# Attention, the sum over the pieces of V in four column groups, and the place at which the maxima are split

## The chip, the cores and the metric

The kernel runs on one core of a Trainium2 chip. Five engines work side by side: TensorE multiplies matrices (PE in the rows; PEld is its weight load), VectorE (DVE), ScalarE (ACT) and GpSimd (POOL) work element by element, and SyncE (SP) issues DMAs. They meet only at semaphores. The metric is the time of one execution on the device in microseconds; several runs give a median.

## What is computed

A layer of linear attention with a normalisation, then a transformer block with softmax attention and a mixture of experts. The change lies in the softmax attention, over 4096 tokens, 16 heads of 16 columns:

```python
scores = jnp.einsum('bqhd,bkhd->bhqk', q, k) / jnp.sqrt(jnp.float32(Dh))
attn = jax.nn.softmax(scores, axis=-1)
ctx = jnp.einsum('bhqk,bkhd->bqhd', attn, v).reshape(Bb, Ss, Dd)
```

(The reference states it for its own batch shape; here it is one sequence of 4096.) The query and key projections are scaled up, so the softmax needs its maxima subtracted, and all of it is done in pieces whose sum is precise.

## The kernel before

`softmax_attention` works through a ring of 128 chunks: 16 heads by 8 chunks of 512 queries. A chunk has 16 slots, one for each unit t; a unit is 128 keys of either half of the keys (k = 0 and 1). Each engine has its own hand-written order, and everything that follows is set by these orders and the semaphores between them.

**TensorE**, in slot t of chunk c: `scores` (L701) makes the scores of unit t, keys by queries, in s_ps (two buffers); `max_pair` (L693) makes scores of chunk c + 2 (LEAD = 2), queries by keys, in two banks of m_ps, only for their maxima; `values` (L720, L726) adds the products of the exponentials with V in o_ps. The visits of `values` lag behind: VISITS and SLOTS say that units 0 and 1 are added in slot 10, unit 3 in slot 12, and so on to unit 15 in slot 24, which is slot 8 of the next chunk. Slots 9 and 11 have no visit. A unit is added either from float32 exponentials (units 3, 6, 9, 12, 15, L720, each matmul in two passes) or from a bfloat16 high part and a float16 low part (L726). The two halves k go to two column groups of 64 in o_ps; each group holds three pieces of V of 16 rows and a row of sums. In slot 11 comes `turn_o` (L735), "the turn" in this text: one float32 matmul, 128 by 128 weights (o_here is the moving data of 512 columns, `gather` the weights), which adds the pieces and both halves up. Its 17 useful rows (16 of the context, one of sums) go to partitions 0 to 16 of m_ps.

**m_ps** has three banks, used in turn: block b, counted over a chunk, uses bank b % 3. The maxima of unit t are blocks 2t and 2t + 1 for t up to 11, the turn is block 24 (TURN_BLOCK), later units come one further. TensorE may write block b when VectorE has read block b - 3.

**VectorE** reads each block of maxima with a reduction (L824); for the units in RELU_PAIRS (2, 5, 8, 12, 15) ScalarE first takes one of the two through a ReLU (L777) and VectorE does the rest in one instruction (L818). Behind slot 11 it copies the turn's result to ctx_stage (L832). In slot 0 it finishes the maxima of the chunk before (tile_max, L839), in slot 6 (FINISH_SLOTS) it transposes their split parts (L842), from which SP fills rows of q_stage.

**ScalarE** takes the exponential of each unit (L790), the ReLUs, and behind slot 8 (COPY_SLOT) copies o_ps to o_here (L781).

**GpSimd** makes the low part of each unit that isn't in FULL_UNITS (L640): 0, 1, 2, 4, 5, 7, 8, 10, 11, 13, 14. MAX_PLACE says ahead of which of them it splits the maxima of the next chunk (L628, L629, L631; `split_max`, which first waits for tile_max): with 2 that is ahead of unit 2. Ahead of the low parts of a head's second chunk it splits V of a later head (`split_v`, L609 to L620); this happens at 14 heads (the first two are done ahead of the ring).

**SP** issues per chunk six loads of queries (L535), 16 row DMAs (L545) once VectorE has transposed, then the two stores of the chunk before (L549, L551), and once per head nine loads of keys.

Of the kernel before, what the change touches and what calls it, by code (L numbers as in the profile page):

```python
# [13 lines left out]
ds = bass.ds  # L14

P = 128
# [3 lines left out]
CHUNK = 512  # L20
CHUNKS = TOKENS // CHUNK
TPC = CHUNK // P
PROJ = 64
HEADS, DH = 16, 16
# [19 lines left out]
O_COLS = DH + 1  # L44
# [6 lines left out]
RING = HEADS * CHUNKS  # L51
Q_BUFS = 4
LEAD = 2
SQ = 32
# [12 lines left out]
COPY_SLOT, TURN_SLOT = 8, 11  # L67
RELU_PAIRS = (2, 5, 8, 12, 15)
FINISH_SLOTS = (0, 6)
MAX_PLACE = 2  # L70
RING_BLOCKS = 2 * UNITS + 1
TURN_BLOCK = 2 * TURN_SLOT + 2
SPLIT_OPS = 5 + len(FULL_UNITS)
# [392 lines left out]
def softmax_attention(nc, dram, keep):  # L466

    with ExitStack() as ctx:
        def sb(name, shape, dt=F32):
            return ctx.enter_context(nc.sbuf_tensor(name, shape, dt))  # L470

        def ps(name, shape, dt=F32):
            return ctx.enter_context(nc.psum_tensor(name, shape, dt))

        def sem(name):
            return ctx.enter_context(nc.semaphore(name))
# [10 lines left out]
        gather = sb("gather", [P, P])  # L487
# [7 lines left out]
        max_parts = sb("max_parts", [P, MROWS, SQ], F32R)  # L495
        max_turned = sb("max_turned", [P, MROWS, SQ])
        o_here = sb("o_here", [P, CHUNK])
        ctx_stage = sb("ctx_stage", [O_COLS, 2, CHUNK])

        s_ps = ps("s_ps", [P, 2, 2, CHUNK])  # L500
        m_ps = ps("m_ps", [P, 3, CHUNK])
# [12 lines left out]
        o_copied, o_turned = sem("o_copied"), sem("o_turned")  # L514
        dve_passed, pool_passed = sem("dve_passed"), sem("pool_passed")
        ctx_out = [sem("ctx_out0"), sem("ctx_out1")]
# [4 lines left out]
        @block.sync  # L521
        def _(sp):
            def load_head(h, par):
                for side, at in ((0, 0), (1, TOP_ROW)):
                    for n, part in enumerate(K_PARTS):
                        sp.dma_start(k_ring[at + DH * n:at + DH * n + DH, ds(par, 1), :].bitcast(F32).rearrange("r a k -> r (a k)"),
                                     dram["ks"][part, ds(h * DH, DH), side, :]).then_inc(head_in, 16)
                for n, part in enumerate(K_PARTS):
                    sp.dma_start(kd_ring[DH * n:DH * n + DH, ds(par, 1), :].bitcast(F32).rearrange("r a k -> r (a k)"),
                                 dram["kd"][part, ds(h * DH, DH), :]).then_inc(head_in, 16)  # L530

            def load_q(h, qc, buf):
                for at in (0, TOP_ROW):
                    for n, part in enumerate(Q_PARTS):
                        sp.dma_start(q_stage[at + DH * n:at + DH * n + DH, ds(buf * CHUNK, CHUNK)].bitcast(F32),  # L535
                                     dram["qs"][part, ds(h * DH, DH), ds(qc * CHUNK, CHUNK)]).then_inc(q_in, 16)

            def rows(n, buf):
                sp.wait_ge(max_ready, n + 1)
                for at in (0, TOP_ROW):  # L540
                    for r in range(MROWS):
                        row = q_stage[at + SROWS + r:at + SROWS + r + 1, ds(buf * CHUNK, CHUNK)].bitcast(F32)
                        row = row.rearrange("a (t b n) -> a t b n", t=TPC, b=P // SQ)
                        for b in range(P // SQ):
                            sp.dma_start(row[:, :, b, :], max_turned[SQ * b:SQ * b + TPC, r, :]).then_inc(rows_in, 16)  # L545

            def store(n, b, h, qc):
                sp.wait_ge(m_read, n * RING_BLOCKS + ((LEAD + 1) * RING_BLOCKS + TURN_BLOCK + 1))
                sp.dma_start(dram["ctx"][ds(qc, 1), ds(h, 1), :, :].rearrange("a b c x -> (a b c) x"),  # L549
                             ctx_stage[0:DH, b, :]).then_inc(ctx_out[b], 16)  # L550
                sp.dma_start(dram["z"][ds(h * CHUNKS + qc, 1), :], ctx_stage[DH:O_COLS, b, :]).then_inc(ctx_out[b], 16)  # L551

            sp.wait_ge(ones_set, 1)
            load_head(sp.snap(0), sp.snap(0))
            for i in range(LEAD + 1):
                load_q(sp.snap(0), i, i)
            rows(0, 0)

            def chunk(h, qc, loads=True, more=True, ahead=True, before=True):

                i = sp.snap(h * CHUNKS + qc)
                if loads:
                    sp.wait_ge(s_done, i * UNITS + 1)
                    n = qc + LEAD + 1
                    load_q(sp.snap(h + n // CHUNKS), n % CHUNKS, n % Q_BUFS)
                    if more and qc == 0:
                        load_head(sp.snap(h + 1), sp.snap((h + 1) & 1))
                if ahead:
                    rows(i + 1, (qc + 1) % Q_BUFS)
                if before:  # L570
                    store(i - 1, 1 - qc % 2, sp.snap(h - 1) if qc == 0 else h, (qc - 1) % CHUNKS)

            for qc in range(CHUNKS):
                chunk(sp.snap(0), qc, before=qc > 0)
            with sp.Fori(1, HEADS - 1) as h:
                for qc in range(CHUNKS):
                    chunk(h, qc)
            for qc in range(CHUNKS):
                chunk(sp.snap(HEADS - 1), qc, loads=qc + LEAD + 1 < CHUNKS, more=False, ahead=qc + 1 < CHUNKS)
            store(RING - 1, 1, sp.snap(HEADS - 1), CHUNKS - 1)  # L580
            for b in range(2):
                sp.wait_ge(ctx_out[b], 32 * (RING // 2))

        @block.gpsimd
        def _(pool):
# [38 lines left out]
            def split_max(n):  # L624

                pool.wait_ge(max_ready, n)
                pool.wait_ge(tile_max_done, n + 1)
                nc.gpsimd.tensor_tensor(neg_max[:, :], no_max[:, :], tile_max[:, :], ALU.subtract).then_inc(max_split, 1)  # L628
                nc.gpsimd.tensor_tensor(max_parts[:, 0, 0:TPC], no_max[:, :], tile_max[:, :], ALU.subtract).then_inc(max_split, 1)  # L629
                pool.wait_ge(max_split, n * 3 + 2)  # L630
                nc.gpsimd.tensor_tensor(max_parts[:, 1, 0:TPC], neg_max[:, :], max_parts[:, 0, 0:TPC].bitcast(F32), ALU.subtract  # L631
                                        ).then_inc(max_split, 1)

            def split_probs(i, more=True):

                for t in POOL_UNITS:
                    if more and t == POOL_UNITS[MAX_PLACE]:
                        split_max(i + 1)
# [32 lines left out]
        def _(pe):  # L671
# [59 lines left out]
            def turn_o(it, c):  # L731

                pe.wait_ge(o_copied, it * PAIR + c)
                pe.wait_ge(m_read, it * (PAIR * RING_BLOCKS) + ((c + LEAD) * RING_BLOCKS + TURN_BLOCK - 2))
                nc.tensor.matmul(m_ps[:, TURN_BLOCK % 3, :], gather[:, :], o_here[:, :], start=True, stop=True  # L735
                                 ).then_inc(o_turned, 1)

            def chunk(it, c, ahead):
                if ahead:
# [25 lines left out]
            for visit, slot in enumerate(SLOTS):  # L765
                if slot >= UNITS:
                    values(HEADS // 2 - 1, PAIR - 1, visit)
            turn_o(HEADS // 2 - 1, PAIR)

        @block.scalar  # L770
# [34 lines left out]
        def _(dve):  # L805
# [21 lines left out]
            def copy_ctx(i, b, stores):  # L827

                dve.wait_ge(o_turned, i)
                if stores is not None:  # L830
                    dve.wait_ge(ctx_out[b], stores * 32)
                nc.vector.tensor_scalar(ctx_stage[:, b, :], m_ps[0:O_COLS, TURN_BLOCK % 3, :], 1.0, None, ALU.mult  # L832
                                        ).then_inc(m_read, 1)

            def finish_max(n, b, step):
# [832 lines left out]
def program(nc, dram):  # L1668
# [6 lines left out]
    with ExitStack() as whole:  # L1675
# [11 lines left out]
        with ExitStack() as through_routing:  # L1687
            keep["v_all"] = right(through_routing, "v_all", [P, TILES, D])
            with ExitStack() as first:
                keep["x_all"] = left(first, "x_all", [P, TILES, D])  # L1690
                linear_attention(nc, dram, keep)
            softmax_attention(nc, dram, keep)
            keep["x_all"] = left(whole, "x1_back", [P, TILES, D])
            output_projection(nc, dram, keep)
            routing(nc, dram, keep)


            keep["w1_in"] = left(whole, "w1_in", [P, HALVES, FF])
            keep["w2_in"] = left(whole, "w2_in", [P, FT, D])
            for name in ("w1_high", "w1_low"):  # L1700
                keep[name] = left(whole, name, [P, 2, HALVES, FT, P], F32R)
            for name in ("w2_high", "w2_low"):
                keep[name] = left(whole, name, [P, 2, FT, D], F32R)
            dispatch(nc, dram, keep)
# [31 lines left out]
```

## Time and profile before

| | |
|---|---|
| runs | 4357.15 us, median of 3 (4355.73 to 4363.25) |
| the profiled execution | 4349.05 us, of which the span is 4347.1 |
| PE busy | 3934.0 us (90%) |
| POOL busy | 3413.5 us (79%) |
| ACT busy | 2829.4 us (65%) |
| DVE busy | 2750.1 us (63%) |
| L735, the turn | 256 passes, mean 686 ns |
| the attention stage | from about 380 to 3472 us of the span |

The span is the time from the first to the last instruction of the profiled execution; what is left of its 4349.05 us lies around it. Times in the rows are microseconds from the start of the span. A row of the order of time gives start, length, engine, line, operation, output and inputs, shapes, the count of merged instructions, and in brackets the idle time ahead of it on its engine with what ended it. Matmuls overlap, so the step from one start to the next is what a matmul costs, and not its own length.

### The profile page before, as it was taken

The page shows a single profiled execution, that of the slowest core. Times are in us where ns is not written, and L with a number is a line of the kernel's source. Part 1 is how long each engine was busy: PE and PEld are TensorE (multiplying, and loading weights), DVE is VectorE, ACT ScalarE, POOL GpSimd, SP SyncE. Part 2 cuts the span into 40 slices and gives each one's busy share as a digit, 9 for nine tenths or more (in the row PEclk, how much of TensorE's full clock was granted, in tenths as well). Part 3 has the DMA queues.
Part 4 walks back from the last instruction along what each step waited for, and adds up shares of the span by engine and source line. Part 5 has one row for each costly group of instructions (what it writes and reads, how often), then busy time and mean ns, then how long its engine had stood idle before and what let it go on. Part 6 is the DMA issues. An engine that isn't in the chain of part 4 may idle for free. (4 is left out here: it accounts for less than half of the span.)

```text
span 4347.1 us, 74722 instructions
## 1 busy us (share of the span) xinstructions
PE 3934.0 (90%) x21172; PEld 1901.6 (44%) x21172; DVE 2750.1 (63%) x5522; ACT 2829.4 (65%) x3421; POOL 3413.5 (79%) x2261
## 2 busy tenths in 40 slices
PE   7469999999999999999999999999999970999990
PEld 4234333333333333333333333333333360899990
DVE  2537777777777777777777777777777451333335
ACT  2125878777787878777787878777788710555550
POOL 0015898989888898988888898988988826888865
PEclk8677999999999999999999999999999975999995
DMA  2241011010101011010101011010100053443434
GB/s 86 111 137 19 11 21 22 10 22 10 22 10 22 10 22 21 11 21 10 22 10 22 10 22 21 11 21 12 20 11 10 17 186 109 140 144 132 147 101 121
DMA packets 145717, 205.12 MB, mean 47 GB/s; under 512 B 43536, under 2 KB 108432, under 8 KB 140176
## 3 DMA queue, kind: packets, MB, share of 16 engines
q1 hardware_dynamic: 127072, 173.76, 14.9%
q0 software_dynamic: 6336, 16.79, 1.2%
q10 hardware_dynamic: 12144, 12.06, 0.8%
q8 instruction: 141, 2.31, 0.2%
q14 instruction: 24, 0.20, 0.0%
HBM read 134.59 MB, written 66.85 MB: 46 GB/s over the span
## 5 line engine op out<-in xcount | busy, mean ns | idle before, releaser
L640 POOL TENSOR_TENSOR probs_low<-probs 128x1024 f16<-128x1024 f32 x1408 | 2632.3, 1894 | 331.0 <-ACT probs L790 324.6
L790 ACT ACTIVATE probs<-s_ps 128x1024 f32<-128x1024 f32 x2048 | 2081.7, 1026 | 240.3 <-PE s_ps L701 190.5
L824 DVE TENSOR_REDUCE unit_max<-m_ps 128x1 f32<-128x512 f32 x2816 | 1779.0, 683 | 222.4 <-PE m_ps L693 181.7
L701 PE MATMUL s_ps<-q_stage,k_ring 50*128 50x512 f32 x4096 | 1043.0, 504 | 1.2 <-DMA q_stage<-max_turned 0.9
L693 PE MATMUL m_ps<-k_ring,q_stage 48*128 48x512 f32 x3456 | 959.5, 424 | 64.3 <-DMA q_stage<-qs_dram 25.4
L701 PEld LDWEIGHTS s_ps<-q_stage,k_ring 50*128 50x128 f32 x4096 | 388.5, 186 | 1160.0 <-issue 907.8
L818 DVE CUSTOM_DVE_ANT_0 excess<-m_ps,excess 128x512 f32<-128x512 f32 x640 | 442.8, 692 | 550.5 <-ACT excess L777 543.9
L720 PE MATMUL o_ps<-probs,v_full 128*64 128x512 f32 x2560 | 698.0, 624 | 0.0
L777 ACT ACTIVATE excess<-m_ps 128x512 f32<-128x512 f32 x640 | 382.1, 597 | 449.8 <-PE m_ps L693 449.8
L726 PE MATMUL o_ps<-probs,v_parts 128*64 128x512 bf16 x2816 | 586.3, 413 | 0.9 <-POOL probs_low L640 0.7
L693 PEld LDWEIGHTS m_ps<-k_ring,q_stage 48*128 48x128 f32 x3456 | 514.8, 192 | 160.5 <-DVE unit_max L824 113.8
L726 PE MATMUL o_ps<-probs_low,v_parts 128*64 128x512 f16 x2816 | 543.2, 383 | 0.0
L1565 DVE TENSOR_TENSOR hidden_low<-h_ps,hidden_high 128x512 fp32r<-128x512 f32 x184 | 127.3, 692 | 365.7 <-ACT hidden_high L1529 365.7
L726 PEld LDWEIGHTS o_ps<-probs,v_parts 128*64 128x64 bf16 x2816 | 156.1, 108 | 379.0 <-issue 304.2
L1525 ACT ACTIVATE h_ps<-h_ps,b_here 128x512 f32<-128x512 f32 x184 | 121.3, 659 | 255.1 <-PE h_ps L1462 255.0
L693 PE MATMUL m_ps<-kd_ring,q_stage 48*128 48x512 f32 x640 | 258.3, 404 | 1.2 <-DVE unit_max L824 1.2
L587 POOL MEMSET k_ring<- 114x4096 f32 x1 | 3.5, 3516 | 293.0 <-POOLq L114 293.0
L1474 PE MATMUL y_ps<-w_low,hidden_high 128*128 128x256 f32 x736 | 209.0, 284 | 0.0
L1474 PE MATMUL y_ps<-w_high,hidden_high 128*128 128x256 f32 x736 | 207.4, 282 | 0.0
L1474 PE MATMUL y_ps<-w_high,hidden_low 128*128 128x256 f32 x736 | 206.6, 281 | 0.0
L720 PEld LDWEIGHTS o_ps<-probs,v_full 128*64 128x64 f32 x2560 | 127.6, 135 | 174.2 <-issue 173.6
L1421 POOL TENSOR_TENSOR w_high<-w_in,zero 128x1024 fp32r<-128x1024 f32 x44 | 130.5, 2983 | 68.3 <-PEq L1493 60.8
(198 smaller groups left out, 3586.6 us busy)
## 6 DMA issues: line engine op xcount, KB each, us to landing
w_in<-in_W SPq DMA_DIRECT2D x46, 1024.0 KB, 4.9
q_stage<-max_turned SPq DMA_DIRECT2D x2048, 0.5 KB
q_stage<-qs_dram SPq DMA_DIRECT2D x768, 32.0 KB, 1.8
k_ring<-ks_dram SPq DMA_DIRECT2D x96, 128.0 KB, 4.2
slots_dram<-zero_rows SPq DMA_DIRECT2D x24, 512.0 KB, 6.3
rows_e<-slots_dram SPq DMA_DIRECT2D x24, 512.0 KB, 3.9
y_slots_dram<-y_out ACTq DMA_DIRECT2D x23, 512.0 KB, 4.3
qs_dram<-parts SPq DMA_DIRECT2D x16, 512.0 KB, 2.8
```

The lines of the kernel that those rows point to most:

```text
L640: nc.gpsimd.tensor_tensor(probs_low[:, LOW_UNITS.index(t), :, :], probs[:, t, :, :], high_view[:, t, :, :, 1], ALU.subtract).then_inc(pool ...
L693: nc.tensor.matmul(m_ps[:, b % 3, :], q_stage[at:at + SROWS, col:col + P], ring[at:at + SROWS, par, key:key + CHUNK], start=True, stop=Tru ...
L701: last = nc.tensor.matmul(s_ps[:, t % 2, k, :], k_ring[at:at + AROWS, par, P * t:P * t + P], q_stage[at:at + AROWS, buf * CHUNK:buf * CHUN ...
L720: last = nc.tensor.matmul(o_ps[V_COLS * k:V_COLS * k + V_COLS, :], v_full[:, par, FULL_UNITS.index(t), k, :], probs[:, t, k, :], start=Fal ...
L726: last = nc.tensor.matmul(o_ps[V_COLS * k:V_COLS * k + V_COLS, :], v_parts[:, par, first_tile(t) + 2 * k, :], part[:, k, :], start=(first ...
L777: nc.scalar.activation(excess[:, :], m_ps[:, block_of(t, 0) % 3, :], ACT.Relu).then_inc(excess_ready, 1)
L790: nc.scalar.activation(probs[:, t, :, :], s_ps[:, t % 2, :, :], ACT.Exp).then_inc(exp_done, 1)
L818: nc.vector.tensor_tensor_reduce(excess[:, :], m_ps[:, block_of(t, 1) % 3, :], excess[:, :], 1.0, LEAST, ALU.add, ALU.max, unit_max[:, b, ...
L824: nc.vector.tensor_reduce(unit_max[:, b, qt, 2 * j + k:2 * j + k + 1], m_ps[:, block_of(t, k) % 3, :], AX.X, ALU.max).then_inc(m_read, 1 + ...
L1421: nc.gpsimd.tensor_tensor(w1_high[:, b, half, :, :], w1[:, half, :, :], zero[:, :].unsqueeze(2).to_broadcast([P, FT, P]), ALU.add).then_in ...
L1474: last = nc.tensor.matmul(y_ps[:, b, t // 2, D * (t % 2):D * (t % 2) + D], h[:, f % 4, cols], w[:, b, f, :], start=(f == 0 and n == 0 and ...
L1565: nc.vector.tensor_tensor(hidden_low[:, f % 4, :], h_ps[:, f % 2, :], hidden_high[:, f % 4, :].bitcast(F32), ALU.subtract).then_inc(low_do ...
```

## The change

MAX_PLACE goes from 2 to 0: GpSimd splits the maxima ahead of the low part of unit 0. The turn becomes four matmuls, each with the first 32 columns of `gather` as weights and a quarter (128 columns) of o_here as data; quarter t goes to the 32 partitions from 32t on. VectorE copies all 128 partitions by 128 columns, and SP stores four pieces of the context and one of the sums (five DMAs in place of two).

```diff
--- before.py
+++ after.py
@@ -67,7 +67,7 @@
 COPY_SLOT, TURN_SLOT = 8, 11
 RELU_PAIRS = (2, 5, 8, 12, 15)
 FINISH_SLOTS = (0, 6)
-MAX_PLACE = 2
+MAX_PLACE = 0
 RING_BLOCKS = 2 * UNITS + 1
 TURN_BLOCK = 2 * TURN_SLOT + 2
 SPLIT_OPS = 5 + len(FULL_UNITS)
@@ -495,7 +495,7 @@
         max_parts = sb("max_parts", [P, MROWS, SQ], F32R)
         max_turned = sb("max_turned", [P, MROWS, SQ])
         o_here = sb("o_here", [P, CHUNK])
-        ctx_stage = sb("ctx_stage", [O_COLS, 2, CHUNK])
+        ctx_stage = sb("ctx_stage", [P, 2, P])
 
         s_ps = ps("s_ps", [P, 2, 2, CHUNK])
         m_ps = ps("m_ps", [P, 3, CHUNK])
@@ -546,9 +546,11 @@
 
             def store(n, b, h, qc):
                 sp.wait_ge(m_read, n * RING_BLOCKS + ((LEAD + 1) * RING_BLOCKS + TURN_BLOCK + 1))
-                sp.dma_start(dram["ctx"][ds(qc, 1), ds(h, 1), :, :].rearrange("a b c x -> (a b c) x"),
-                             ctx_stage[0:DH, b, :]).then_inc(ctx_out[b], 16)
-                sp.dma_start(dram["z"][ds(h * CHUNKS + qc, 1), :], ctx_stage[DH:O_COLS, b, :]).then_inc(ctx_out[b], 16)
+                for t in range(TPC):
+                    sp.dma_start(dram["ctx"][ds(qc, 1), ds(h, 1), :, P * t:P * t + P].rearrange("a b c x -> (a b c) x"),
+                                 ctx_stage[SQ * t:SQ * t + DH, b, :]).then_inc(ctx_out[b], 16)
+                sp.dma_start(dram["z"][ds(h * CHUNKS + qc, 1), :].rearrange("a (t x) -> (a t) x", t=TPC),
+                             ctx_stage[DH:P:SQ, b, :]).then_inc(ctx_out[b], 16)
 
             sp.wait_ge(ones_set, 1)
             load_head(sp.snap(0), sp.snap(0))
@@ -579,7 +581,7 @@
                 chunk(sp.snap(HEADS - 1), qc, loads=qc + LEAD + 1 < CHUNKS, more=False, ahead=qc + 1 < CHUNKS)
             store(RING - 1, 1, sp.snap(HEADS - 1), CHUNKS - 1)
             for b in range(2):
-                sp.wait_ge(ctx_out[b], 32 * (RING // 2))
+                sp.wait_ge(ctx_out[b], 16 * (TPC + 1) * (RING // 2))
 
         @block.gpsimd
         def _(pool):
@@ -732,8 +734,10 @@
 
                 pe.wait_ge(o_copied, it * PAIR + c)
                 pe.wait_ge(m_read, it * (PAIR * RING_BLOCKS) + ((c + LEAD) * RING_BLOCKS + TURN_BLOCK - 2))
-                nc.tensor.matmul(m_ps[:, TURN_BLOCK % 3, :], gather[:, :], o_here[:, :], start=True, stop=True
-                                 ).then_inc(o_turned, 1)
+                for t in range(TPC):
+                    last = nc.tensor.matmul(m_ps[SQ * t:SQ * t + SQ, TURN_BLOCK % 3, 0:P], gather[:, 0:SQ],
+                                            o_here[:, P * t:P * t + P], start=True, stop=True)
+                last.then_inc(o_turned, 1)
 
             def chunk(it, c, ahead):
                 if ahead:
@@ -828,8 +832,8 @@
 
                 dve.wait_ge(o_turned, i)
                 if stores is not None:
-                    dve.wait_ge(ctx_out[b], stores * 32)
-                nc.vector.tensor_scalar(ctx_stage[:, b, :], m_ps[0:O_COLS, TURN_BLOCK % 3, :], 1.0, None, ALU.mult
+                    dve.wait_ge(ctx_out[b], stores * (16 * (TPC + 1)))
+                nc.vector.tensor_scalar(ctx_stage[:, b, :], m_ps[:, TURN_BLOCK % 3, 0:P], 1.0, None, ALU.mult
                                         ).then_inc(m_read, 1)
 
             def finish_max(n, b, step):
```

## Rows read from the trace of the kernel before

**Rows 1.** The page: granted TensorE clock in 40 slices of the span, in tenths.
```profile
PEclk8677999999999999999999999999999975999995
```

**Rows 2.** Order of time, the turns of three chunks.
```profile
401.24 1.12 PE L735 MATMUL m_ps<-o_here,gather 128*128 128x512 f32 x2
...
567.17 1.12 PE L735 MATMUL m_ps<-o_here,gather 128*128 128x512 f32 x2
...
3297.20 1.13 PE L735 MATMUL m_ps<-o_here,gather 128*128 128x512 f32 x2
```

**Rows 3.** Windows: stretch, length, busy PE, PEld, DVE, ACT, POOL (instructions), clock, DMA share, GB/s.
```profile
1519.57:1543.31 23.74, 23.60 (x132) 9.26 (x131) 18.08 (x35) 19.10 (x23) 21.04 (x15) 1.00 0.41 61
1543.31:1571.27 27.96, 26.34 (x132) 10.48 (x131) 18.17 (x35) 19.51 (x23) 25.70 (x24) 0.90 0.04 9
...
1565.40:1572.30 6.90, 6.90 (x24) 2.99 (x22) 3.50 (x8) 3.56 (x4) 6.90 (x4) 0.51 0.01 1
...
2716.70:2742.50 25.80, 23.87 (x132) 9.47 (x130) 18.15 (x35) 19.18 (x23) 23.54 (x23) 1.00 0.04 10
```

**Rows 4.** Order of time, a head's second chunk, POOL, then DVE, then PE.
```profile
1558.86 3.74 POOL L640 TENSOR_TENSOR probs_low<-probs 128x1024 f16<-128x1024 f32 x2 [0.40 <-POOL v_parts L620]
...
1562.57 0.20 POOL L628 TENSOR_TENSOR neg_max<-no_max,tile_max 128x4 f32<-128x4 f32 x1
...
1559.58 1.29 DVE L824 TENSOR_REDUCE unit_max<-m_ps 128x1 f32<-128x512 f32 x2
...
1563.23 0.24 DVE L842 STREAM_TRANSPOSE max_turned<-max_parts 128x64 f32<-128x64 f32 x1 [2.36 <-POOL max_parts L631]
...
1564.11 0.49 PE L693 MATMUL m_ps<-k_ring,q_stage 48*128 48x512 f32 x1 [1.62 <-DVE unit_max L824]
```

**Rows 5.** Line L842, 540 to 3330 us: idle before it (us, times).
```profile
  POOL max_parts L631: 33.2, 14
```

**Rows 6.** Order of time on PE, slots 8 to 12 of an ordinary chunk.
```profile
1538.69 1.08 PE L720 MATMUL o_ps<-probs,v_full 128*64 128x512 f32 x4
...
1541.65 0.41 PE L726 MATMUL o_ps<-probs,v_parts 128*64 128x512 bf16 x2
...
1542.99 0.39 PE L693 MATMUL m_ps<-k_ring,q_stage 48*128 48x512 f32 x2
1543.31 1.13 PE L735 MATMUL m_ps<-o_here,gather 128*128 128x512 f32 x2
1544.37 0.51 PE L701 MATMUL s_ps<-q_stage,k_ring 50*128 50x512 f32 x2
1544.70 0.39 PE L693 MATMUL m_ps<-kd_ring,q_stage 48*128 48x512 f32 x1
```

**Rows 7.** Order of time, slot 0 of the same chunk, POOL, then DVE.
```profile
1528.38 3.75 POOL L640 TENSOR_TENSOR probs_low<-probs 128x1024 f16<-128x1024 f32 x2 [0.44 <-ACT probs L790]
...
1528.62 0.17 DVE L839 TENSOR_REDUCE tile_max<-unit_max 128x4 f32<-128x32 f32 x1
```

**Rows 8.** Order of time on PE, eight transposes in the stage of the experts.
```profile
3736.63 1.04 PE L1454 MATMUL tr_ps<-ident,rows_e 128*128 128x128 f32 x8
```

**Rows 9.** Order of time, slots 10 to 12, DVE, then PEld.
```profile
1543.41 1.29 DVE L824 TENSOR_REDUCE unit_max<-m_ps 128x1 f32<-128x512 f32 x2 [0.45 <-PE m_ps L693]
1544.62 0.67 DVE L832 TENSOR_SCALAR ctx_stage<-m_ps 17x512 f32<-17x512 f32 x1
...
1541.22 0.18 PEld L693 LDWEIGHTS m_ps<-k_ring,q_stage 48*128 48x128 f32 x1 [0.57 <-DVE unit_max L824]
...
1544.76 0.18 PEld L693 LDWEIGHTS m_ps<-k_ring,q_stage 48*128 48x128 f32 x1
```

**Rows 10.** Order of time on SP's queue, end of a chunk's issues.
```profile
1547.51 0.34 SPq L549 DMA_DIRECT2D ctx_dram<-ctx_stage  x1
1548.06 0.24 SPq L551 DMA_DIRECT2D z_dram<-ctx_stage  x1
1551.06 0.35 SPq L535 DMA_DIRECT2D q_stage<-qs_dram  x1
```

## The prediction

> **What bounds the kernel now.** I read the page first: TensorE (PE) is the busiest engine by far (the table above), and its line of granted clocks stands at 9 for nearly the whole attention stage, where 9 may be anything below full speed [rows 1]. The change touches that stage only, so next I timed its period: the turn (L735) comes once per chunk and marks it. From the first row of turns to the second there are 7 chunks: (567.17 - 401.24) / 7 = 23.71 us. From the second to the third there are 112 chunks: 2730.03 us, where 112 x 23.71 would be 2655.5 [rows 2]. So 74.5 us are lost somewhere in those 112 chunks. The windows show where: an ordinary chunk takes 23.7 us at clock 1.00, but the chunk that begins at 1543.31 takes 27.96 at clock 0.90 [rows 3]. There are 14 such places, one for each head whose V GpSimd splits inside the loop (every eighth chunk), and nothing is lost elsewhere.
>
> What happens there is a wait behind a wait [rows 4]. GpSimd has just split V (its first low part is released by its own v_parts), runs two low parts (3.74 us) and only then splits the maxima, from 1562.57. VectorE has finished its reductions of unit 6 at 1559.58 + 1.29 = 1560.87 and sits until 1563.23 for max_parts (2.36 us idle). Its next reduction frees a bank of m_ps, so TensorE's second matmul of pair 8 comes only at 1564.11, after 1.62 us idle. The wait of VectorE occurs exactly 14 times, 33.2 us in all [rows 5]. Behind the stall the granted clock is half (0.51) for 6.9 us [rows 3], that is 1.2 instead of 2.4 GHz. One of the 14 kept its clock: its chunk took 25.80 us [rows 3], 2.1 over the period. So the stall costs 2.1 us, 14 x 2.1 = 29, and the clock that falls behind it 74.5 - 29 = 45 us.
>
> **The change, part by part.** (1) *The split of the maxima ahead of the first low part.* In a head's second chunk two low parts no longer stand before it. GpSimd was ready for new work at 1558.86; from the first of the three small subtractions, at 1562.57, to VectorE's start behind the last, at 1563.23, it is 0.66 us; so max_parts is there for VectorE at about 1559.5, and VectorE asks for it at 1560.87 [rows 4]. Margin 1.4 us: the wait of 2.36 us goes, and with it the stall of 1.62. What is late next? GpSimd's low parts 0 and 1, which now end at 1558.86 + 0.6 + 3.74 = 1563.2. TensorE wants them at slot 10. In the chunk before, this visit began at 1541.65 [rows 6], so here, a period of 23.71 later, it begins at 1565.4: 2.2 us to spare. Gain: the 29 us of stalls, and, if the clock falls because of them, the 45 us too. That it does is borne out by the order: each fall follows such a stall, and no other chunk between 567 and 3297 us shows one.
>
> In the other chunks the split now waits for tile_max. GpSimd begins its first low part at 1528.38, tile_max is there at 1528.62 + 0.17 = 1528.79 [rows 7]; with 0.6 us of splitting the first low part begins near 1529.4, 1.0 us later. Behind it on GpSimd stand the other low parts; the one who waits for the first two is TensorE's visit in slot 10, 13 us later [rows 6, 7]. GpSimd works 21.04 of 23.74 us in a chunk [rows 3] and catches up in its pauses before the chunk is over. Cost 0. No DMA is moved.
>
> (2) *The turn.* Now it is one matmul in two passes, and from its start at 1543.31 to the next scores at 1544.37 it takes 1.06 us [rows 6]. The new form is four matmuls of 32 columns of weights by 128 columns of data, eight passes. If the column groups run beside each other, two passes of 128 columns are left: a quarter of 1.06, 0.27, and at most 0.1 for eight starts, about 0.35 us. If they run one after the other: eight passes of 128 by 128 columns took 1.04 us from the first start to the last end [rows 8], the turn's two 1.13 in the same measure [rows 6]; 1.0 us. I take 0.35, since the two column groups of L720 do four passes of 512 in 1.08 us, where the turn needs 1.13 for two [rows 6]. It hardly matters, because of what comes next.
>
> The Trainium skill, "TensorEngine Tiling (Array Packing)", section "Key Properties", says that different tiles can load weights and multiply in parallel, but that changing the mode drains the engine. By the first half the turn falls to a quarter; by the second it pays a drain on each side, as the turn before already does between row-tiled matmuls. The sum below is the same by either.
>
> 0.7 us less per chunk would be 127 x 0.7 = 89 us, if TensorE set the pace there. It doesn't. Behind the turn come the scores of slot 12 and its pair of maxima, and the second matmul of that pair takes its bank only when VectorE has read block 23. VectorE's two reductions run 1543.41 + 1.29 = 1544.70; the weight load of that second matmul starts at 1544.76, 0.06 behind, while the first of the pair had started at 1544.70 without it [rows 6, 9]. The same 0.05 stands between a reduction and the weight load at 1541.22, where the trace names VectorE as the releaser (0.57 us idle) [rows 9]. So today the turn exactly fills a gap in which TensorE would otherwise wait. VectorE's two reductions begin when the maxima of slot 11 are there, ahead of the turn in TensorE's order; a shorter turn doesn't move them. With a turn of 0.35 us the scores and the first matmul come 0.6 to 0.7 earlier, the second at 1544.76 as before. Gain 0 per chunk; cost 0 as long as the turn stays under 1.06 + 0.05 us.
>
> (3) *VectorE's copy* goes from 512 to 128 elements per partition; today 0.67 us [rows 9]. It stands behind block 23, before a reduction that waits for ScalarE. Between nothing and 0.5 us of VectorE's time per chunk, off the path: 0.
>
> (4) *Stores.* Five DMA issues instead of two. Today the last issue ends at 1548.06 + 0.24 = 1548.30 and SP's next work is at 1551.06 [rows 10]. An issue steps by about 0.55 (1547.51 to 1548.06), so three more end at 1549.95: hidden. They stand behind the 16 row DMAs, so TensorE's rows aren't moved. If the cover went, the loads of queries that follow are for three chunks ahead. Only after the last chunk is it bare: +1.7 us, against 0.7 of the turn, up to 0.5 of the copy, and up to 0.7 in each of the last two turns, which have no maxima beside them: 0 to within 2 us.
>
> **Sum.** Profiled execution: 4349.05 us (span 4347.1). 4349.05 - 74.5 = 4274.6. The median of the runs, 4357.15, lies 8.1 higher; single heads lose 2.1 to 9 us in the trace, so a part of these 8.1 is probably more of the same loss. If all of it goes, 4274.6; if none, 4282.7. I take the middle, 4279.
>
> **The rivals.**
> *A: the clock falls in ordinary chunks; slower.* The turn is dense work that now becomes a wait. In each chunk TensorE already waits 0.6 us in slot 10; with 0.7 more in slot 12 some 1.3 us would be idle within 4 us, close to the 1.62 behind which the clock fell 13 times of 14. A fall costs 45 / 13 = 3.5 us on the mean, a light one 27.96 - 25.80 = 2.2 [rows 3]. From 74.5 / 2.2 = 34 light falls in 127 chunks on the change loses; one in every second chunk gives 4279 + 64 x 2.2 = 4420. Against it: the waits lie apart with matmuls between, and chunks with only the 0.6 never fell. 8%. The Trainium skill, "TensorE: Matmul & The Clock Gate", section "A second HAM failure mode: psum-queue depth-cycling", describes this: short pauses between groups of matmuls, from waiting for PSUM banks, let the clock swing. The trace so far shows one pause per chunk without that.
> *B: only the stalls go, the clock falls come with the change of head for another reason:* 4357 - 29 = 4328. For it: they have the same beat. Against it: the one that didn't fall, and that each comes behind the stall. 7%.
> *C: nothing gained:* something else in a head's second chunk is late, for instance GpSimd's backlog of the V split now holds TensorE's visits (margins of 2.2 us above). 4357. 6%.
> *D: the turn does more than fill the gap:* the four groups take over 1.11 us, for instance 0.3 over it: +38, 4317. The rows of eight passes speak against it. 6%.
> *E: the turn's 0.7 us reaches the period* because VectorE's reductions also come earlier: down to 4279 - 89 = 4190. 5%.
>
> **How the numbers follow.** The forecast has 68%: 4268 to 4292. B and D reach up to 4330; leaving out A, C and E (19%) gives the range 4262 to 4332. A difference of about 0.2% (9 us) is what a measurement here can tell. Faster: 68 + 7 + 6 + 5 = 86%, same: C, 6%, slower: A, 8%.
>
> **What would show it.** After: no wait of VectorE's transpose for max_parts; no half clock between 567 and 3230 us; all turns 23.71 us apart, those at heads too; a turn of 0.3 to 0.5 us, and behind it a new wait of TensorE for VectorE of 0.6 to 0.7 us at the second maximum of slot 12, with a total of TensorE's waits for unit_max up by 80 to 90 us. The prediction is wrong if the period of an ordinary chunk moves from 23.71 at all, up (A, D) or down (E), or if one chunk in eight still is longer (B, C).

## The result and the profile after

The changed kernel takes 4285.26 us (median of 4 runs, 4279.53 to 4287.82), the kernel before beside it 4356.44 (4353.59 to 4363.25). The ratio is 0.9833, with a 95% interval from 0.9816 to 0.9850: 71 us less, where 78 were forecast (4279). The profiled execution takes 4279.53 us, its span 4277.5.

First the granted clock in 40 slices, on the page of the changed kernel. The 9s of the attention stage that had stood for small losses in [rows 1] are the same digits, so the page alone doesn't show where the time went; the windows of three chunks below do, the first of them one in which GpSimd splits V.

```profile
PEclk8687999999999999999999999999999965999995
```

Windows of the changed kernel: stretch, length, busy PE, PEld, DVE, ACT, POOL, granted clock, DMA share, GB/s. The turns (L738 now) of this head stand at 1515.5, 1539.2, 1562.9 and 1586.6.

```profile
1515.50:1539.20 23.70, 23.46 (x138) 9.17 (x136) 17.68 (x35) 19.09 (x23) 21.38 (x22) 1.00 0.04 11
1539.20:1562.90 23.70, 23.48 (x138) 9.18 (x136) 17.67 (x35) 19.11 (x23) 23.62 (x16) 1.00 0.05 11
1562.90:1586.60 23.70, 23.48 (x138) 9.21 (x136) 17.70 (x35) 19.09 (x23) 23.62 (x17) 1.00 0.04 11
```

The first holds GpSimd's split of V (22 of its instructions instead of 15). It is the answer to the chunk of 27.96 us at clock 0.90 in [rows 3], and takes 23.70 at clock 1.00. The period itself, 23.7, hasn't moved. The waits of the transpose (line L842 before, L846 now), and the order of time around it, tell why:

```profile
  POOL max_parts L633: 0.9, 1
```
```profile
1529.48 1.16 POOL L622 TENSOR_TENSOR v_parts<-v_rest,v_parts 128x512 bf16<-128x512 f32 x1
1531.10 0.20 POOL L630 TENSOR_TENSOR neg_max<-no_max,tile_max 128x4 f32<-128x4 f32 x1 [0.46 <-POOL v_parts L622]
1531.25 0.20 POOL L631 TENSOR_TENSOR max_parts<-no_max,tile_max 128x4 fp32r<-128x4 f32 x1
1531.54 0.20 POOL L633 TENSOR_TENSOR max_parts<-neg_max,max_parts 128x4 fp32r<-128x4 f32 x1
...
1532.94 0.23 DVE L846 STREAM_TRANSPOSE max_turned<-max_parts 128x64 f32<-128x64 f32 x1
```

33.2 us of wait at 14 heads [rows 5] are 0.9 us once, at the last transpose of the ring (3350.10), away from every change of head. GpSimd splits the maxima right behind V and is done at 1531.74; VectorE comes for them at 1532.94, 1.2 us later.

Now the turn. The source view of its line, first in the kernel before and then in the changed one (shortest, median, longest in ns; first and last start in us), and after it the order of time around one turn of the changed kernel, PE, PEld, DVE:

```profile
L735 PE MATMUL m_ps<-o_here,gather x256: 592/697/1220, 401.2 to 3468.6; 128*128 128x512 f32 x128
```
```profile
L738 PE MATMUL m_ps<-o_here,gather x1024: 272/285/298, 401.0 to 3393.2; 128*32 128x128 f32 x171
```
```profile
1538.88 0.40 PE L695 MATMUL m_ps<-k_ring,q_stage 48*128 48x512 f32 x2
1539.21 0.43 PE L738 MATMUL m_ps<-o_here,gather 128*32 128x128 f32 x8
1539.56 0.49 PE L703 MATMUL s_ps<-q_stage,k_ring 50*128 50x512 f32 x2
1540.06 0.50 PE L695 MATMUL m_ps<-kd_ring,q_stage 48*128 48x512 f32 x1
1540.66 0.49 PE L695 MATMUL m_ps<-k_ring,q_stage 48*128 48x512 f32 x1
1541.08 1.08 PE L722 MATMUL o_ps<-probs,v_full 128*64 128x512 f32 x4
...
1540.06 0.18 PEld L695 LDWEIGHTS m_ps<-kd_ring,q_stage 48*128 48x128 f32 x1 [0.31 <-DVE unit_max L828]
1540.66 0.18 PEld L695 LDWEIGHTS m_ps<-k_ring,q_stage 48*128 48x128 f32 x1 [0.41 <-DVE unit_max L828]
...
1539.31 1.29 DVE L828 TENSOR_REDUCE unit_max<-m_ps 128x1 f32<-128x512 f32 x2 [0.46 <-PE m_ps L695]
1540.52 0.28 DVE L836 TENSOR_SCALAR ctx_stage<-m_ps 128x128 f32<-128x128 f32 x1
```

The turn steps by 1539.56 - 1539.21 = 0.35 us where it stepped by 1.06 [rows 6]. From its start to the second maximum of slot 12 it is 1540.66 - 1539.21 = 1.45 us; before it was 1544.76 - 1543.31 = 1.45 [rows 6, 9]. The 0.7 us turned into two waits for VectorE on the way, at 1540.06 and 1540.66; VectorE's two reductions end at 1540.60, 0.06 ahead of the second weight load. Over the ring, the wait of TensorE's weight loads for VectorE's reductions (total, times, longest), before and after:

```profile
PEld m_ps L693 <- DVE unit_max L824: 100.1, 138, 2.1
```
```profile
PEld m_ps L695 <- DVE unit_max L828: 159.9, 374, 0.6
```

Of the 100.1 us some 29 belong to the 14 stalls (14 x 2.1), so the ordinary waits went from 71 to 160, up by 89; the prediction named 80 to 90.

The last turn starts 75.4 us earlier than before (3468.6 to 3393.2), of which 0.2 were there at the first; so the ring of chunks gave 75.2. The span is shorter by 69.6. So 5.8 us came back behind the last turn, where 878.5 us before (4347.1 - 3468.6) are 884.3 now. Other profiles show that this stretch differs by as much without any change in it: it is 886.9 in a second profile of the changed kernel (c1), 882.8 in e1 and 878.1 in e3, both with the stores as before. The five stores are not needed to explain the 5.8.

### The profile page after: what moved, and what is told of

The parts are those of the page before. It is cut to its first block and busy times, and to the rows that moved or that the text cites. A ratio compares the mean times of both kernels' runs of the same rounds, so it can differ in the third digit from the quotient of the medians.

```text
span 4277.5 us, 77314 instructions
## 1 busy us (share of the span) xinstructions
PE 3864.1 (90%) x21940; PEld 1873.1 (44%) x21940; DVE 2698.7 (63%) x5522; ACT 2826.9 (66%) x3421; POOL 3404.0 (80%) x2261
## 5 line engine op out<-in xcount | busy, mean ns | idle before, releaser
L703 PE MATMUL s_ps<-q_stage,k_ring 50*128 50x512 f32 x4096 | 1031.1, 498 | 1.2 <-DMA q_stage<-max_turned 0.9
L695 PE MATMUL m_ps<-k_ring,q_stage 48*128 48x512 f32 x3456 | 944.8, 418 | 55.6 <-DMA q_stage<-qs_dram 25.4
L695 PEld LDWEIGHTS m_ps<-k_ring,q_stage 48*128 48x128 f32 x3456 | 506.2, 188 | 169.9 <-DVE unit_max L828 135.1
L695 PE MATMUL m_ps<-kd_ring,q_stage 48*128 48x512 f32 x640 | 270.3, 422 | 1.2 <-DVE unit_max L828 1.2
```

Source lines behind the costliest of these rows:

```text
L695: nc.tensor.matmul(m_ps[:, b % 3, :], q_stage[at:at + SROWS, col:col + P], ring[at:at + SROWS, par, key:key + CHUNK], start=True, stop=Tru ...
L703: last = nc.tensor.matmul(s_ps[:, t % 2, k, :], k_ring[at:at + AROWS, par, P * t:P * t + P], q_stage[at:at + AROWS, buf * CHUNK:buf * CHUN ...
```

## The experiments

My theory in step with the prediction: all the gain comes from the place of the split, by way of a stall and a clock that falls behind it; the short turn is hidden. The rivals: the turn gives a part, the clock falls with the head, the less dense work costs.

**e1, the place alone.**
```diff
-MAX_PLACE = 2
+MAX_PLACE = 0
```


> Edit: MAX_PLACE 0 in the kernel before, turn and stores as before. My theory (the stall of VectorE behind GpSimd's late split costs 2.1 us at each of 14 heads and the fall of the clock behind it the rest): the whole gain of the change, 71 to 75 us, so 4282 to 4286 us, and no half clock between 400 and 3300 us. Rival 'the turn gives the gain': 4357, at least half of the gain missing. Rival 'the clock falls with the change of head, not with the stall': 29 us of gain, 4328, half clock still at every eighth chunk.

Measured: 4282.51 us (4278.56 to 4285.36) against 4344.52 of the kernel before beside it, ratio 0.9855 (0.9836 to 0.9874). The head's window, again with the split of V in it:

```profile
1519.20:1542.90 23.70, 23.56 (x132) 9.26 (x130) 18.06 (x35) 19.11 (x23) 21.38 (x22) 1.00 0.04 11
```

Neither stall nor low clock is left, with the long turn. The rival of the clock that falls with the head is out, and within the interval so is the one of the turn: the absolute time is that of the changed kernel (4285.26 and, below, 4288.30). The kernel before was 12 us faster in this measurement, so the ratio shows less gain. Its eight times spread over 13.5 us, those of e1 over 6.8, and its mean granted clock goes with them (0.935 at 4340.39 us, 0.931 at 4353.86): what it loses to the low clock differs from one execution to the next.

**e2, the turn alone** (the changed kernel with the old place).
```diff
-MAX_PLACE = 0
+MAX_PLACE = 2
```


> Edit: the changed kernel with MAX_PLACE back at 2, so the turn in four column groups, VectorE's smaller copy and the five stores alone. My theory: 4357, within 0.2%, since the 0.7 us saved at the turn come back as a wait at the second maximum of slot 12; heads cost 4.6 us and more as before, 13 or 14 falls of the clock. Rival 'the turn gives a part': up to 89 us less, 4268. Rival 'less dense work lets the clock fall more often': above 4365.

Measured: 4381.00 us (4366.97 to 4390.63), ratio 1.0074 (1.0050 to 1.0098): slower, by 32 us by the ratio. I had expected no change; the rival of the less dense work was right in its sign. VectorE's wait for max_parts is there as before:

```profile
  POOL max_parts L633: 38.3, 15
```

and the ordinary chunk is still 23.7 us. The loss is at the heads, in the chunk behind the stalled one. Windows, first two of the kernel before (1543.31 stands in [rows 3]), then three of e2, the stalled chunk first:

```profile
1571.30:1595.30 24.00, 23.88 (x132) 9.25 (x130) 18.17 (x35) 18.86 (x23) 22.72 (x16) 0.98 0.05 11
1595.30:1619.00 23.70, 23.58 (x132) 9.25 (x130) 18.06 (x35) 19.12 (x23) 21.07 (x15) 1.00 0.05 11
```
```profile
1548.00:1575.60 27.60, 25.86 (x142) 10.10 (x140) 17.78 (x35) 19.45 (x23) 25.33 (x24) 0.91 0.04 9
1575.60:1604.00 28.40, 28.26 (x138) 10.28 (x136) 17.75 (x35) 18.87 (x23) 23.19 (x16) 0.78 0.04 9
1604.00:1627.70 23.70, 23.49 (x138) 9.19 (x136) 17.69 (x35) 19.09 (x23) 21.04 (x15) 1.00 0.05 11
```

At this head of the kernel before, the clock is back at full speed for nearly all of the chunk behind (0.98). With the short turn that chunk runs at 0.78 and costs 4.4 us more. Over the whole ring, from turn to turn, the stalled chunks and those behind them take 74.7 us more than ordinary ones in the trace before and 104.2 in e2, and TensorE is at half clock for 116 and 195 us. Why was asked of e5.

**e3, the place between.**
```diff
-MAX_PLACE = 2
+MAX_PLACE = 1
```


> Edit: MAX_PLACE 1 in the kernel before. GpSimd's split then comes one low part (1.87 us) later than with 0, so at a head's second chunk VectorE waits 1.87 - 1.38 = 0.5 us. Before, 2.36 us of VectorE's wait became 1.62 of TensorE's, a slack of 0.74. My theory: a wait of 0.5 us lies inside that slack, TensorE doesn't stall, the clock doesn't fall: the same time as with 0, 4282 to 4286. Rival 'any late split costs': 14 x 0.5 = 7 us more than with 0. Rival 'falls come with the head': as for e1.

Measured: 4279.69 us (4279.46 to 4282.38), ratio 0.9851 (0.9833 to 0.9868). The transpose's waits, and the head's window between two ordinary ones:

```profile
  POOL max_parts L631: 11.1, 15
```
```profile
1494.80:1518.50 23.70, 23.56 (x133) 9.25 (x131) 18.06 (x35) 19.11 (x23) 21.06 (x15) 1.00 0.40 61
1518.50:1542.50 24.00, 23.68 (x133) 9.51 (x131) 18.15 (x35) 19.10 (x23) 21.74 (x22) 1.00 0.05 11
1542.50:1566.20 23.70, 23.56 (x132) 9.22 (x130) 18.06 (x35) 19.10 (x23) 23.62 (x16) 1.00 0.05 11
```

VectorE waits some 0.7 us per head (11.1 over 15), a little more than the 0.5 worked out, and the chunk takes 0.3 us more, 4 us over 14 heads, which the times can't tell. The clock doesn't fall. Place 1, with one low part ahead of the split instead of two, would have been enough for the gain within what can be measured.

**e4, the split late in every chunk.**
```diff
-MAX_PLACE = 2
+MAX_PLACE = 6
```


> Edit: MAX_PLACE 6 in the kernel before, so that the split is late in every chunk: its end moves four low parts (7.5 us) back, from 1532.7 to about 1541, against VectorE's need at 1537.06, a wait of some 3.7 us for VectorE and 2.9 us for TensorE in each ordinary chunk. My theory (a stall brings the clock down, wherever it is): half clock in most of the 127 chunks, 2.9 + 2 to 3.5 us more for each, 4357 + 620 to 810 = 4980 to 5170. Rival 'the clock falls with the head only': 4357 + 370 = 4727, and half clock no more often than before.

Measured: 5263.61 us in one run, above the range expected. Two windows of ordinary chunks, and the stalled matmul of the second:

```profile
1505.00:1535.75 30.75, 28.08 (x130) 10.70 (x130) 18.25 (x35) 19.32 (x22) 21.08 (x15) 0.83 0.04 8
1535.75:1566.40 30.65, 28.09 (x130) 10.70 (x130) 18.27 (x35) 19.30 (x22) 21.00 (x14) 0.83 0.04 8
...
1567.53 0.79 PE L693 MATMUL m_ps<-k_ring,q_stage 48*128 48x512 f32 x1 [2.67 <-DVE unit_max L824]
```

No change of head is near, the stall is 2.67 us (2.9 expected), and the clock falls in each chunk: a stall brings it down wherever it stands. I had the price of the fall too low: of the 7.0 us over the period about 3 are stall and 4 the clock. At the mean of 0.83 a third of each chunk runs at half speed, 10 us, where one head's stall gave 6.9 [rows 3].

**e5, the short turn three times over,** made of e2, so with the old place.
```diff
-                for t in range(TPC):
+                for t in 3 * tuple(range(TPC)):
                     last = nc.tensor.matmul(m_ps[SQ * t:SQ * t + SQ, TURN_BLOCK % 3, 0:P], gather[:, 0:SQ],
```


> Edit: e2_turn_only with the short turn's four matmuls issued three times over (24 passes, the same result written again), so that TensorE's pause behind the turn is filled with about as much work (3 x 0.34 us) as the long turn had. In e2 the low clock behind a head's stall lasted 17 to 24 us at most heads instead of 7 to 17, and that made it 0.7% slower than before. My theory (the turn's work had helped the clock to come back, and the pause in its place delays it): back to the time of the kernel before, within 0.3% of it (about 4350 on this kind of chip), low clock of 7 to 17 us at the heads. Rival 'the smaller copy or the five stores cost the 30 us': as e2, 0.7% over the kernel before.

Measured: 4352.07 us (4335.66 to 4369.87, 10 runs), the kernel before 4342.97, ratio 1.0018 (0.9995 to 1.0041): not to be told from no change, and 0.56% better than e2. A head of it, the stalled chunk and the one behind:

```profile
1544.40:1572.30 27.90, 26.26 (x144) 10.83 (x144) 16.82 (x33) 17.95 (x22) 26.50 (x24) 0.82 0.04 10
1572.30:1596.70 24.40, 24.26 (x158) 9.67 (x156) 18.24 (x36) 19.89 (x23) 21.85 (x15) 1.00 0.05 10
```

The copy and the five stores are as in e2, the ordinary period too. The stalled chunk and the one behind it take 52.3 us here, 56.0 in e2 and 52.0 before (27.96 + 24.00). Over the ring the chunks at the heads take 58.4 us more than ordinary ones, with 82 us at half clock. This profile flatters e5, since it is the shortest of its ten times, and that of e2 is one of its longer ones; but the mean granted clock of all executions says the same: the median is 0.923 in e2, 0.930 in e5 and 0.933 in the kernel before. So what delays the clock's return is that TensorE has less work at the turn; the copy and the stores are not.

Whether it is the pause or the smaller amount of work isn't shown. In e2, PE around the turn that falls into the low clock:

```profile
1575.58 0.65 PE L738 MATMUL m_ps<-o_here,gather 128*32 128x128 f32 x8
...
1576.76 0.62 PE L695 MATMUL m_ps<-kd_ring,q_stage 48*128 48x512 f32 x1
1577.03 0.79 PE L695 MATMUL m_ps<-k_ring,q_stage 48*128 48x512 f32 x1
```

At half clock TensorE's pause behind the short turn is only about 0.3 us, since its other work there takes longer and VectorE's does not. e5 fills that pause and adds work besides: at half clock its turn steps by 1.44 us (1568.97 to 1570.41), that of e2 by 0.58 (1575.58 to 1576.16). How long the clock stays low still varies from head to head in all three kernels, 7 to 24 us where it falls; it falls at 13 heads before, 11 in e2 and 10 in e5.

**The changed kernel again, and a new spacing.** If VectorE's reading of block 23 (the second block of maxima in slot 11) swallowed the turn's gain, the gain should appear once TensorE has other work between the maxima of slots 11 and 12. c1 is the changed kernel, o1 the new spacing with the short turn, o2 with the long one (on e1).

> The changed kernel itself, for comparison with the next two on one chip. 4280 to 4288 us, period 23.71 us; behind the shorter turn TensorE waits for VectorE at the second maximum of slot 12.

```diff
-VISITS = ((0, 1), (3,), (2,), (4,), (6,), (5,), (7,), (9,), (8,), (10,), (12,), (11,), (13, 14), (15,))
-SLOTS = (10, 12, 13, 14, 15, 16, 17, 18, 19, 20, 21, 22, 23, 24)
-COPY_SLOT, TURN_SLOT = 8, 11
+VISITS = ((0, 1), (3,), (2,), (4,), (6,), (5,), (7,), (9,), (8,), (10,), (12,), (11,), (13,), (14,), (15,))
+SLOTS = (10, 11, 12, 13, 14, 15, 16, 17, 18, 19, 20, 21, 22, 23, 24)
+COPY_SLOT, TURN_SLOT = 8, 10
```


> Edit: the changed kernel with the visit of units 13 and 14 taken apart and every visit behind the first one slot earlier (slots 10 to 24 one each, none free but slot 9), and the turn behind slot 10 in place of 11. The order of the additions into o_ps is otherwise the same. In slot 11 TensorE then has 1.0 us of products between the maxima of slot 11 and those of slot 12, which VectorE needs to read its two blocks. My theory (VectorE's reading of block 23 swallowed the turn's gain): the wait of 0.85 us in slot 12 goes, period 22.86 us, 127 x 0.85 = 108 us less, 4174 us. Rival 'another engine (GpSimd at 21.0 us of work per chunk and 7 us per head, or ScalarE) takes over as soon as the period falls': 4240 or more. Rival 'the wait only moves to the next slot': 4282.

> Edit: the same new spacing with the long turn of the kernel before (and its copy and two stores), MAX_PLACE 0. My theory: here TensorE sets the pace all through the turn, so the long turn costs its 0.7 us in each chunk: 0.7 x 127 = 89 us over the short one, 4263 us, period 23.56. Rival 'the turn's form is hidden in any order': the same time as with the short one.

Measured: c1 4288.30 us, at the edge of what was expected, ratio 0.9855 (0.9829 to 0.9880); o1 4321.74, 0.9927 (0.9901 to 0.9953); o2 4404.17, 1.0120 (1.0094 to 1.0146). Both respaced kernels are slower than forecast, by 148 and 141 us, and slower than c1 and e1; but they differ by 82 us, 0.65 us for each of 127 chunks: there the short turn counts. What held them up, in o1's waits over 1500 to 2500 us (total, times, longest), and the same view of the changed kernel:

```profile
PEld s_ps L703 <- ACT probs L794: 215.9, 374, 0.8
```
```profile
PEld s_ps L703 <- ACT probs L794: 63.6, 142, 0.8
```

The scores wait for ScalarE's exponentials. The float32 visits of 1.0 us had stood in the slots in which ScalarE also has a ReLU (2, 5, 8, 12, 15); I had moved the visits and left the ReLUs.

**The ReLUs moved along.** o3 is o1, o4 is o2, with one more line:
```diff
-RELU_PAIRS = (2, 5, 8, 12, 15)
+RELU_PAIRS = (1, 4, 8, 11, 14)
```


> Edit: o1_respaced_short with RELU_PAIRS (1, 4, 8, 11, 14) in place of (2, 5, 8, 12, 15). In o1 the wait of slot 12 was gone, but the long visits (L722) had moved to slots 1, 4, 11, 14, away from the ReLUs of slots 2, 5, 12, 15, and ScalarE, with a ReLU in a short slot, held the scores up by 0.3 us in slots 14, 1 and 4 and in slot 10. With the ReLUs in the long slots again my theory gives what was expected of o1: period 22.9 to 23.0, 4174 to 4190 us. Rival 'ScalarE or GpSimd can't keep a shorter period anyway': 23.5 or more, 4260 or more.

> Edit: the same as o3 with the long turn of the kernel before (its copy and stores too). o1 and o2 already differed by 0.69 us a chunk. My theory: here too, 0.7 us a chunk and 80 to 90 us over o3, 4260 to 4275. Rival 'VectorE sets the pace again': the same as o3.

Measured: o3 4189.31 us (4185.20 to 4191.21), ratio 0.9637 (0.9606 to 0.9668); o4 4273.98 (4268.83 to 4278.52), ratio 0.9837 (0.9805 to 0.9869). Between them 84.7 us, 0.67 a chunk. The order of time on PE around a turn, o3 first, then o4:

```profile
1526.47 0.50 PE L695 MATMUL m_ps<-k_ring,q_stage 48*128 48x512 f32 x1 [0.23 <-DVE unit_max L828]
...
1527.89 0.42 PE L738 MATMUL m_ps<-o_here,gather 128*32 128x128 f32 x8
1528.25 0.49 PE L703 MATMUL s_ps<-q_stage,k_ring 50*128 50x512 f32 x2
1528.58 0.40 PE L695 MATMUL m_ps<-kd_ring,q_stage 48*128 48x512 f32 x1
1528.59 0.40 PE L695 MATMUL m_ps<-k_ring,q_stage 48*128 48x512 f32 x1
```
```profile
1534.23 0.50 PE L693 MATMUL m_ps<-k_ring,q_stage 48*128 48x512 f32 x1 [0.20 <-DVE unit_max L824]
...
1535.66 1.13 PE L735 MATMUL m_ps<-o_here,gather 128*128 128x512 f32 x2
1536.71 0.50 PE L701 MATMUL s_ps<-q_stage,k_ring 50*128 50x512 f32 x2
1537.05 0.40 PE L693 MATMUL m_ps<-kd_ring,q_stage 48*128 48x512 f32 x1
1537.06 0.40 PE L693 MATMUL m_ps<-k_ring,q_stage 48*128 48x512 f32 x1
```

In both, the two matmuls of the pair behind the turn now start together, with no wait for VectorE; so the turn's 0.36 and 1.05 us count in full. The waits of 0.23 and 0.20 us in slot 10, ahead of the turn, are left in both.

o3 takes 96 us less than the changed kernel (median 4285.26) and 3.6% less than the kernel before. The spacing alone gives little: o4, with the long turn, has the ratio 0.9837 (0.9805 to 0.9869) where e1 has 0.9855 (0.9836 to 0.9874), which is within the noise. Neither the short turn nor the new order is worth much by itself; together they are.

## Why the prediction was right

**Where the 74.5 us were lost**, at 14 changes of head, and by what, a stall and the clock behind it: confirmed by e1 (gone with the stall), e3 (a short wait, no fall) and e4 (a stall in every chunk, a fall in every chunk). The ring gave 75.2 us against 74.5 forecast; the difference is rounding, since the period by the prediction's own rows is 23.704 and not 23.71 us, which makes the loss 75.2 too. One reading was too narrow: "nothing is lost elsewhere" holds only if the chunk behind is counted with the stalled one. From turn to turn the 14 stalled chunks took 25.85 to 29.13 us, and at 13 heads the chunk behind took 23.98 to 29.02. The sum doesn't rest on it. Rival B is out: with e1 no clock falls at a head.

**The margins.** 1.4 us for max_parts was 1.2; GpSimd's backlog held nobody (the window behind the head is 23.70 at 23.62 us of GpSimd's work). Rival C is out.

**The first low part later in every chunk**: cost 0, as said; the period is 23.7.

**The turn**: 0.35 us forecast, 0.35 measured; eight passes of four column groups run beside each other, and rival D is out. That it gains nothing, because VectorE's reading sets the second maximum of slot 12, holds to the hundredth: 1.45 us on either side. The form in which the wait showed was not quite the one forecast: one wait of 0.6 to 0.7 us was expected at the second matmul, and there are two, since the first of the pair already waits for block 22. Rival E is out for this order; o3 and o4 show what it takes to make it true.

**VectorE's copy** fell from 0.67 to 0.28 us, off the path.

**The stores** were mis-sized, without harm. I took 0.55 us a step, which left 1.1 us to spare (1551.06 - 1549.95). SP's queue of the changed kernel:

```profile
1543.76 1.85 SPq L550 DMA_DIRECT2D ctx_dram<-ctx_stage  x4
1545.79 0.62 SPq L552 DMA_DIRECT2D z_dram<-ctx_stage  x1
1546.94 2.69 SPq L535 DMA_DIRECT2D q_stage<-qs_dram  x6
```

The five take 1546.41 - 1543.76 = 2.65 us where two took 0.79 [rows 10]; the store of the sums, now from four partitions 32 apart, issues in 0.62 instead of 0.24. They are over 0.5 us before the next loads, which begin as long after the turn as before (1546.94 - 1539.21 = 7.73 us, 1551.06 - 1543.31 = 7.75).

**Rival A**, the slower one, was half a warning. With the stalls gone the clock falls in no ordinary chunk, so the waits in each chunk are not enough to bring it down. But where it had fallen behind a stall, the short turn kept it down longer (e2: 195 us at half clock over the ring, against 116). The change is safe because both halves came together; the turn alone cost 0.7%. The prediction had priced the turn at nothing, and that holds only while the clock is full.

**The size.** 4279 was forecast, 4285.26 measured, 6.3 us more. The profiled execution took 4279.5 where 4274.6 was forecast: the ring gave 0.7 us more than was summed, 0.2 were there ahead of it, and 5.8 came back behind it. The median lies 5.7 us above the profiled execution, where the middle of the prediction's two cases took 4.4; that choice cost 1.3 us. The 5.8 us are no more than the stretch behind the ring differs between two profiles (878.1 to 886.9 us in the four named above), so no cause can be given for them.

## What to carry to other kernels

Time the period of a regular kernel from one marked instruction to the next and subtract the ordinary period from the whole: what is left over is lost at a few places, and here it was all the gain. Before shortening an operation on the busiest engine, look at the next instruction behind it that shares a buffer with another engine: if its start follows close behind that engine's end (0.05 us here), the operation may only fill a gap, and the order must be respaced first (with all that was tuned to the old order, here the ReLUs). A short stall of TensorE can cost two or three times its length when the clock falls behind it (here 74.5 / 14 = 5.3 us a head for a stall of 1.62, and 7.0 a chunk for 2.67 in e4), and work taken from TensorE for no gain at full clock can cost time while the clock is low.

## What the runs showed that was not expected

- A stall of 1.62 us brought TensorE's clock from 2.4 to 1.2 GHz for about 6.9 us and more at 13 of 14 heads [rows 3, 4]; one of 2.67 us in each chunk brought it down each time, for about 10 us (e4); waits of 0.3 and 0.4 us in one chunk (the changed kernel) never did.
- Work that is of no use brought the clock back sooner: e5 issues the turn three times and is 0.56% better than e2 (ratios 1.0018 and 1.0074), with 82 us at half clock over the ring in its profile against 195.
- Eight float32 passes of 32 by 128 columns in four column groups took 0.35 us from start to next work at 2.4 GHz, a third of the 1.06 us of two passes of 128 by 512.
